# A graph layer with a mixture of experts on one core: statistics moved, matmuls of constants added, small tables relocated

## The reference

```python
xn  = layernorm(x)
h   = einsum('ni,roi->rno', xn, weight)            # 8 relations
x   = x + segment_sum(h[edge_type, src], dst) + bias
xn2 = layernorm(x)
p   = softmax(xn2 @ gate_w + gate_b)               # 16 experts
top 2 of p, normalised to sum 1                    # per node
x   = x + sum over the two: p_e * ((silu(xn2 @ w1[e]) * (xn2 @ w2[e])) @ w3[e])
```

## Time and profile before

| | us |
|---|---|
| three runs | 925.81, 927.80, 933.22 (median 927.8) |
| the profiled execution | 927.84 |
| its span | 926.1 |
| PE busy | 725.9 (78%) |
| POOL busy | 659.9 (71%) |
| DVE busy | 520.1 (56%) |
| ACT busy | 300.0 (32%) |

### The profile page before, as it was taken

How to read it: one execution, slowest core, us unless ns; L and a number is a source line. 1 busy time by engine, 2 the same in 40 slices (tenths; PEclk the granted TensorE clock), 3 DMA queues, 4 the chain that set the end, 5 groups by cost and what they waited for, 6 DMA issues and landing times.

```text
span 926.1 us, 17827 instructions
## 1 busy us (share of the span) xinstructions
PE 725.9 (78%) x4528; PEld 617.5 (67%) x4529; DVE 520.1 (56%) x1447; ACT 300.0 (32%) x466; POOL 659.9 (71%) x614
## 2 busy tenths in 40 slices
PE   0135778888887898877889887388999999999980
PEld 0123567666776677766777666267888888888870
DVE  6687746465454654546554577883444444344438
ACT  5423233252222433234332333222333333233323
POOL 7774777777777777777777760249788796987772
PEclk9997799899998999989999999589999999999995
DMA  9872444454444433343334334166756664763546
GB/s 207 245 224 63 146 145 145 144 178 145 144 144 137 133 104 103 106 130 107 102 106 131 106 95 147 34 203 236 222 186 227 205 197 167 229 210 95 158 135 188
DMA packets 91487, 141.91 MB, mean 153 GB/s; under 512 B 13197, under 2 KB 65889, under 8 KB 91456
## 3 DMA queue, kind: packets, MB, share of 16 engines
q0 software_dynamic: 25680, 70.16, 26.2%
q1 hardware_dynamic: 48854, 56.28, 18.9%
q10 hardware_dynamic: 16922, 15.15, 5.1%
HBM read 108.61 MB, written 32.93 MB: 153 GB/s over the span
## 4 chain that ended last, share of the span: by engine, by line
PE 39%; POOL 25%; issue 17%; DMA 11%; DVE 3%; ACT 2%; SPq 1%; DVEq 1%; POOLq 0%; ACTq 0%
POOL got L573 21%; PE ps L1677 15%; PE ps L1659 8%; PE ps L1525 8%; DMA got<-x_tab,gidx 5%; PE ps L1537 5%; DMA acc<-in_x 2%; PE ps L1685 2%; POOL x_sb L618 2%; DMA store<-in_L_gnn_weight 2%; PE ps L1643 1%; DVE ps L1450 1%; POOL part L607 1%; DMA y_tab<-ffn 1%; DMA x_tab<-x_sb 1%
## 5 line engine op out<-in xcount | busy, mean ns | idle before, releaser
L573 POOL DMA_INDIRECT got<-x_tab,gidx x388 | 370.9, 956 | 127.1 <-issue 113.1
L1525 PE MATMUL ps<-hot,got 125*128 125x256 f16 x1700 | 222.0, 292 | 88.3 <-DMA got<-x_tab,gidx 69.7
L1525 PEld LDWEIGHTS ps<-hot,got 125*128 125x128 f16 x1700 | 172.9, 104 | 133.2 <-issue 45.9
L1095 DVE TENSOR_TENSOR store<-store,ps 128x512 f32 x150 | 102.6, 684 | 187.8 <-PE ps L1525 153.2
L1677 PE MATMUL ps<-part,operands 128*128 x696 | 180.7, 409 | 5.3 <-POOL part L607 4.1
L1537 PE MATMUL ps<-part,store 128*128 128x256 f32 x800 | 183.7, 388 | 0.5 <-DVE acc L1106 0.5
L1537 PEld LDWEIGHTS ps<-part,store 128*128 128x128 f32 x800 | 154.0, 195 | 21.0 <-issue 0.5
L1677 PEld LDWEIGHTS ps<-part,operands 128*128 128x128 f32 x696 | 129.6, 193 | 33.4 <-issue 6.1
L1077 DVE TENSOR_SCALAR hot<-key_row,pass,drel 125x256 f16<-125x256 f16 x425 | 124.4, 358 | 11.2 <-issue 11.1
L1659 PE MATMUL ps<-part,operands 128*128 x696 | 97.8, 289 | 3.2 <-DVE operands L1389 3.2
L607 POOL TENSOR_TENSOR part<-store,part 128x2048 fp32r<-128x2048 f32 (+1 forms) x28 | 98.0, 3499 | 2.3
(11 more groups left out here) (250 smaller groups left out, 658.0 us busy)
## 6 DMA issues: line engine op xcount, KB each, us to landing
store<-in_L_ffn_w SPq DMA_DIRECT2D x48, 512.0 KB
y_tab<-ffn SPq DMA_DIRECT2D x9, 896.0 KB, 4.5
y_tab<-ffn ACTq DMA_DIRECT2D x58, 128.0 KB
xs_tab<-x_sb SPq DMA_DIRECT2D x14, 512.0 KB, 3.2
ffn<-xs_tab ACTq DMA_DIRECT2D x55, 128.0 KB
got<-x_tab,gidx POOLq DMA_INDIRECT x388, 2.7
acc<-in_x SPq DMA_DIRECT2D x5, 560.0 KB
x_tab<-got SPq DMA_DIRECT2D x5, 560.0 KB
```

The source lines that it names most:

```text
L573: nc.gpsimd.indirect_dma_start(got[:, c, :], None, x_tab, bass.IndirectOffsetOnAxis(ap=gidx[:, col:col + 1], axis=0)).then_inc(gathered[g] ...
L1095: v.tensor_tensor(window, window, ps[:, WIN_BANK[g], :].rearrange("p (q n) -> p q n", n=WIN), ALU.add).then_inc(win_added, 1)
L1525: last = mm(ps[:, WIN_BANK[g], k * KEYS:(k + 1) * KEYS], got[0:CE, c, a * DIM + k * P:a * DIM + (k + 1) * P], hot[0:CE, g % HOT, c - c0, : ...
```

## The change

1. The 37 early gathers raise three semaphores: `held_in[0]` for the first ten, `[1]` for the next fifteen, `[2]` for the twelve of the odd turns. DVE takes the statistics of the first ten (`held_moments(0)`) and then `edge_keys()` ahead of `statistics(3)`; the other two parts stay where all 37 stood.
2. ACT, not DVE, copies the two lines of ends and the keys out of PSUM (semaphore `lines_kept`), behind its rows of x. DVE waits for the lines before it works on them and for the keys before L1033.
3. ACT takes the two square roots of the held rows in the midst of its eight copies of turned weights, behind the fourth, and waits there for all 37 variances (`held_var`).
4. DVE reads its counts into registers behind the held variances, ahead of its wait for these square roots.
5. `held_low(v0)` of the first turn of a sweep stands behind the first three windows' adds.
6. PE multiplies constants (`ones_h` with `key_row`, 128x128 by 128x256 float16, into a PSUM bank that nothing reads) at four places of routing: 28, 28, 20 and 22 times (`keep_clock`).
7. `oct_tables` stands behind the first tile's product; the rows `upto`, `upto_i` and `need` (now `slots_needed`) stand together ahead of the second tile's product; the result's weights and `pos2` stand behind the second tile.

```diff
+SOON = 10
+HELD_PARTS = (0, SOON, TILES, EARLY)
...
-                    bass.IndirectOffsetOnAxis(ap=early_idx[:, t:t + 1], axis=0)).then_inc(held_in, 16)
+                    bass.IndirectOffsetOnAxis(ap=early_idx[:, t:t + 1], axis=0)).then_inc(held_in[(t >= SOON) + (t >= TILES)], 16)
...
+            turned = "p (j q) -> p j q"
+            act.wait_ge(edges_turned, 2)
+            for n, ends_line in enumerate((lo_line, hi_line)):
+                nc.scalar.copy(ends_line.rearrange("p (q j) -> p j q", j=EJ),
+                               ps[0:1, 2 + n, 0:CHUNKS].rearrange(turned, j=EJ)).then_inc(lines_kept, 1)
+            nc.scalar.copy(key_c[0:CE, :].rearrange("p (q j) -> p j q", j=EJ),
+                           ps[0:CE, 1, 0:CHUNKS].rearrange(turned, j=EJ)).then_inc(lines_kept, 1)
+
             for n in range(8):
                 k, rp = n // 4, n % 4
                 act.wait_ge(w_turned, n + 1)
                 nc.scalar.copy(wT[:, k, rp * QW:(rp + 1) * QW], ps[:, 5 + n % 3, :]).then_inc(wT_ready, 1)
+                if n == 3:
+                    act.wait_ge(held_var, EARLY)
+                    nc.scalar.activation(dev[0:CE, :], mv[0:CE, :, 1], ACT.Sqrt, bias=eps[0:CE, 1:2], scale=SCALE ** -2).then_inc(held_dev, 1)
+                    nc.scalar.activation(odd_dev[0:CE, :], odd_mv[0:CE, :, 1], ACT.Sqrt, bias=eps[0:CE, 1:2], scale=SCALE ** -2).then_inc(held_dev, 1)
...
+            def held_moments(part):
+
+                t0, t1 = HELD_PARTS[part:part + 2]
+                dve.wait_ge(held_in[part], (t1 - t0) * 16)
+                for t in range(t0, t1):
+                    n = t - TILES
+                    v.bn_stats((stat[0:CE, t, :] if n < 0 else odd_stat[0:CE, n, :]),
+                               (held[0:CE, t, :] if n < 0 else odd_held[0:CE, n, :])).then_inc(held_stats, 1)
+                for t in range(t0, t1):
+                    n = t - TILES
+                    dve.wait_ge(held_stats, t + 1)
+                    v.bn_aggr((mv[0:CE, t, :] if n < 0 else odd_mv[0:CE, n, :]),
+                              (stat[0:CE, t, :] if n < 0 else odd_stat[0:CE, n, :])).then_inc(held_var, 1)
+
...
             for n in range(1, X_LOADS):
+                if n == 3:
+                    held_moments(0)
+                    edge_keys()
                 statistics(n)
-                if n == 3:
-                    edge_keys()
...
-            step(v.tensor_copy(key_c[0:CE, :].rearrange("p (q j) -> p j q", j=EJ), ps[0:CE, 1, 0:CHUNKS].rearrange(turned, j=EJ)))
-            for n, ends_line in enumerate((lo_line, hi_line)):
-                step(v.tensor_copy(ends_line.rearrange("p (q j) -> p j q", j=EJ), ps[0:1, 2 + n, 0:CHUNKS].rearrange(turned, j=EJ)))
+            dve.wait_ge(lines_kept, 2)
...
+            held_moments(1)
+            held_moments(2)
+            dve.wait_ge(counts_ready, 5)
...
+            tiles_n = dve.value_load(n_tiles[0:1, 0:1], min_val=1, max_val=TILES)
...
             dve.wait_ge(held_dev, 2)
...
-                    held_low(v0)
                     for g in range(HALF):
                         one_hots((g + HOT_AHEAD) // NG, (g + HOT_AHEAD) % NG)
                         add_window(v0, 0, g, w, 0, offs)
+                    held_low(v0)
...
+            def keep_clock(n):
+
+                for _ in range(n):
+                    mm(ps[:, IDLE_BANK, 0:KEYS], ones_h[:, :], key_row[:, :], start=True, stop=True)
+
+            keep_clock(28)
             pe.wait_ge(hots_done, 1)
             ranks(FIRST_PART, TILES).then_inc(ranks_done, 1)
+            keep_clock(28)
             pe.wait_ge(own_summed, 1)
...
+            keep_clock(20)
             by_hots = ([(k, t) for k in range(2) for t in range(HOT_TILES)] + [(k, t) for k in range(2) for t in range(HOT_TILES, TILES)])
...
             last.then_inc(inv_summed, 1)
+            keep_clock(22)
             pe.wait_ge(upto_kept, 2)
```

The tables between the expert tiles on DVE; `slots_needed` and `result_weights` hold the instructions that stood at L1415 to L1419 with L1436 to L1440, and at L1422 to L1433 with L1441:

```diff
                 if not first:
                     low_hid(j - 1)
+                    if tables:
+                        tables()
...
                 v.tensor_tensor(hid, gate, ps[:, UP_BANK + 1, :], ALU.mult).then_inc(hid_ready, 1)
+                if first and tables:
+                    tables()
                 low_xs(j + 1)
...
             split_first(0, (DOWN_PART,))
-            oct_tables()
-            expert_tile(0, 0, first=True)
+            expert_tile(0, 0, first=True, tables=oct_tables)
             split_first(1, (UP_PARTS, DOWN_PART))
-            expert_tile(0, 1)
+            expert_tile(0, 1, tables=slots_needed)
+            result_weights()
             expert_tile(1, 0)
             expert_tile(1, 1)
```

More of the change, by code:

```diff
@@ L286, in build @@
         early_rows = sem("early_rows")
-        early_turned = sem("early_turned")
         early_ready = sem("early_ready")
-        held_in = sem("held_in")
+        held_in = [sem(f"held_in{n}") for n in range(3)]
+        lines_kept = sem("lines_kept")
         held_stats = sem("held_stats")
@@ L989, in _ @@
                 low_row(t)
-            dve.wait_ge(edges_turned, 1)
+            dve.wait_ge(edges_turned, 2)
             turned = "p (j q) -> p j q"
@@ L1043, in _ @@
             v.memset(limit[:, :], 0.0).then_inc(edges_done, 1)
-            dve.wait_ge(held_in, EARLY * 16)
-            for t in range(EARLY):
-                n = t - TILES
-                v.bn_stats((stat[0:CE, t, :] if n < 0 else odd_stat[0:CE, n, :]),
-                           (held[0:CE, t, :] if n < 0 else odd_held[0:CE, n, :])).then_inc(held_stats, 1)
-            for t in range(EARLY):
-                n = t - TILES
-                dve.wait_ge(held_stats, t + 1)
-                v.bn_aggr((mv[0:CE, t, :] if n < 0 else odd_mv[0:CE, n, :]),
-                          (stat[0:CE, t, :] if n < 0 else odd_stat[0:CE, n, :])).then_inc(held_var, 1)
+            held_moments(1)
+            held_moments(2)
+            dve.wait_ge(counts_ready, 5)
+            dve.wait_ge(edges_done, 1)
+            dve.wait_ge(acc_init, 1)
+            dve.wait_ge(bias_kept, 1)
+            tiles_n = dve.value_load(n_tiles[0:1, 0:1], min_val=1, max_val=TILES)
+            wins_n = dve.value_load(n_wins[0:1, 0:1], min_val=1, max_val=GEN_W)
+            single = dve.value_load(single_i[0:1, 0:1], min_val=0, max_val=1)
+            visits = dve.value_load(n_visits[0:1, 0:1], min_val=TILES, max_val=TILES * TILES * GEN_W)
             dve.wait_ge(held_dev, 2)
@@ L1390, in low_hid, with expert_tile @@
                                 hidT[:, 0, :, :].bitcast(F32), ALU.subtract).then_inc(hidT_ready, 1)
-            def expert_tile(i, u, first=False):
+            def expert_tile(i, u, first=False, tables=None):
                 j = i * 2 + u
@@ L1409, in _ @@
             split_first(0, (DOWN_PART,))
-            oct_tables()
-            expert_tile(0, 0, first=True)
-            split_first(1, (UP_PARTS, DOWN_PART))
-            expert_tile(0, 1)
-            dve.wait_ge(upto_kept, 2)
-            TILE_ROW = [1, TILES, EXPERTS]
-            for k in range(2):
-                step(v.tensor_tensor(mine, upto_tile, bc(same[:, EXPERTS - 2 + k, :], TILE_ROW, 1), ALU.mult))
-                step(v.tensor_reduce(upto[:, k, :], mine, AX.X, ALU.add))
-            expert_tile(1, 0)
@@ L1429, in _ @@
-            step(v.tensor_tensor(wts[:, 1, :], wts[:, 1, :], wts[:, 0, :], ALU.mult))
-            for k in range(2):
-                v.tensor_tensor(wts2[:, k, :], wts[:, 0, :], is_low[:, k, :], ALU.mult)
-                step(v.tensor_tensor(mtx[:, :], wts[:, 1, :], is_low[:, 1 - k, :], ALU.mult))
-                step(v.tensor_tensor(wts2[:, k, :], wts2[:, k, :], mtx[:, :], ALU.add))
-            expert_tile(1, 1)
-            step(v.tensor_scalar(upto_i[:, :, :], upto[:, :, :], float(P - 1), None, ALU.add))
```

55 lines of the change are left out of this document (29 added, 26 removed).

## The result

The changed kernel took 919.12 us (median of 4 runs), the kernel before 927.45 beside it: a ratio of 0.9886, 95% interval 0.9859 to 0.9913. Predicted were 917.9 with a range of 915.0 to 922.0. One of the four runs took 937.93 at a lower granted clock (0.835, where the others had 0.93); the ratio leaves it out, and the other three have a median of 918.04. The profiled execution took 918.04, its span is 916.3; before they were 927.84 and 926.1.

What follows compares the result with a forecast made beforehand. POOL's stream of gathers was taken to bound the graph stage, with one hole of 9.17 us to close. 927.84 - 9.2 (hole) - 0.4 (constants) - 0.3 (tables) = 917.9 us, range 915.0 to 922.0.

Steps and rivals of the forecast that it cites:

- Ten statistics, "free": DVE's preparation: ten early held statistics, 4.1 us, fit its wait for batch 3; edge keys bring later rows 1.0 forward.
- Copies on ACT: Preparation: three copies, 2.75 us, leave DVE, which waits 0 for ACT and is 3.7 early with the edge keys' 1.0.
- Held rows at 65.2: DVE's preparation: the other 27 held rows take 6.1 and 4.9 us, ending at 65.2 and not 73.6.
- Square roots and DVE's loads: Preparation: DVE's 2.9 us of register loads run beside ACT's roots; ACT waits up to 1.0; clear ends at 73.4.
- Start of PE, 70.2: PE's first window starts at 70.2 through DVE's chain, against 71.1 needed; the hole closes, gain 9.17 us.
- Matmuls of constants, +0.4: Routing: constants raise PE's clock, 0.4 us won at the inverse table; ends 1.5 lost and 0.5 won.
- Rival C: Routing's first 28 constants at half clock: hole closed, DVE waits 1.5 for ranks, 920.1 us; chance 0.15 with E.
- Tables, +0.3: Expert stage: moved tables spare PE's idle before the seventh tile; 1.3 could be won, 1 lost; 0.3 us taken.
- A: Preparation: hole closes only in part, PE starts at 72 to 74, gain 6 to 8, 921 us; chance 0.20.
- B: Routing and experts: hole closes, clock stays full through the seventh tile's product, table early, 916.8 us; chance 0.12.
- D: Preparation: slower, DVE waits for ten gathers; decides if the tenth lands from 34.4, 935.4 us at 42; chance 0.03.
- E: Routing: clock stays at half despite the constants, only 0.4 and 0.3 go, 918.6 us; chance 0.15 with Rival C.

Runs made afterwards that it cites:

- ten_late_again: Changed kernel with the first ten held statistics back among the others, edge keys still ahead of batch 3, measured a second time: 920.77 us, ratio 0.9912.
- no_constants: Changed kernel without its 98 matmuls of constants: 918.30 us, ratio 0.9893 to the kernel before.
- reads_early: Changed kernel with PE's two register loads moved ahead of its turning of the weights: 918.74 us, ratio 0.9897 to the kernel before.
- old_tables: Changed kernel with the small tables at their places of before: 918.15 us, ratio 0.9897 to the kernel before.
- routing_only: Kernel before with only the matmuls of constants and the relocated tables: 929.58 us, ratio 1.0002 to the kernel before.

## Why the prediction was right

The forecast was 917.9 and the time 919.1 (918.0 without the long run). The main term, the hole in POOL's stream, is most of what was won: 7.5 of the 9.8 us of the span. That the sum came out within 0.1 in the span (916.2 and 916.3) is in part luck: the hole closed by 7.5 and not by 9.2, the constants and tables brought 0.1 and not 0.7 that can be traced to them, and what fills the gap are the 0.64 by which POOL's own first turn ended early and the 1.2 behind the first routed gather, neither of which the sum had. Point by point:

*The bound.* Right. POOL's stream of gathers sets the graph stage and the hole was the one thing in it to win. Where it closed fully (three kernels) the time is no better than where 1.35 were left: such a difference is less than the spread between runs of one kernel. From POOL's second turn to the choice pass 493.8 to 496.6 us in the eight traces, whatever the edits.

*Ten statistics, "free".* Partly wrong. The tenth gather landed at 25.4, not at 23.6, so that ten statistics and edge keys (7.0) ran to 32.4, past batch 3 at 29.75. "I take 1.0" for the rows behind it was 0.4 by the copy of the index (45.15 to 44.77). The upper bound, 2.0, is about what `ten_late_again` got by leaving the ten out (42.74, 2.4 early). The net worth of the ten is 1.8 at DVE, not 4.1, and they cost the issue of the weights' load 2.0.

*Copies on ACT.* Right: DVE waited 0.23 for them, and was 3.1 early at L1027 (49.01 to 45.90, with the 0.4), against 3.7 predicted.

*Held rows at 65.2.* 65.3 in the trace. DVE began them at 54.6 and not 54.2, and the 27 took 10.7 instead of 11.0.

*Square roots and DVE's loads.* Predicted was a wait of up to 1.0 on ACT for the variances. There was none, because the weights landed at 62.5. In `no_constants`, with a landing at 61.45, the fourth copy ends within 0.2 of the last variance (65.75 and 65.58). DVE's four loads took 2.18, not 2.9, and its one-hots began at 68.26, with no 0.3 for the head of the loop: by DVE alone PE could have started at 69.4. The clear ended at 75.09, not at 73.4, and "no one-hot does" need it is wrong: in DVE's queue the wait for it (L1262) stands ahead of the one-hots of the fourth group. In `reads_early` DVE idled 3.34 there and PE 1.65 in its first turn; POOL's gathers show no gap from it.

*Start of PE, 70.2.* It was 71.84, 70.43, 70.44 in the three executions with that preparation. The chain I named, through DVE, is not the one that decides; the other does: "PE's own two register loads stand behind the last copy ... 67.8 + 1.5 = 69.3, earlier". From the last copy to PE pass 2.33, not 1.5, and the last copy ended at 69.5, not at 67.8. `reads_early` shows the first: with only these loads moved, PE starts 1.1 nearer to the last copy (1.24 instead of 2.33) and waits for DVE. The second is the landing, 2.7 later than the 59.8 that the sum implies: issued 0.4 and not 1.0 early, and 16.7 underway where I had kept the 14.7 of before. In the eight traces this load took 13.8 to 16.7; with 14.7, by my estimate, PE would have started at 69.8 (45.75 + 14.7 + 9.3), or at 70.2 if ACT then waits for the variances, and the hole would have closed. So this part of the miss is chance. The hole's limit moved too: POOL's first turn ended 0.64 early, so that PE had to start by 70.5 and not by 71.1. 70.43 and 70.44 closed the hole, in `old_tables` with 0.1 to spare, and 71.84 left 1.35. The hole's term was 7.5 in the profiled execution (9.17 to 1.65), inside the ends 7.2 and 9.17 but 1.7 short of what I took.

*Matmuls of constants, +0.4.* The saving of 0.34 at the table is there in four executions of six, but the first 28 found the clock at half in every execution (4.88 to 6.01 us) and delayed the ranks by 0 to 0.85. Together, from the choice to `first_idx`, that is up to 0.3 won in five executions and 0.8 lost in one, so the term is near nil. Rival C's mechanism, half clock at the first 28, is what happens, at up to 0.85 instead of 1.5, and belonged in the forecast.

*Tables, +0.3.* The full clock at the seventh tile came, and is worth 1.3 in that product (4.34 to 3.04), but `old_tables` and `no_constants` have it as well. The 1.2 won behind the first routed gather are in all variants (0.8 to 1.8), in `routing_only` too, which is no faster than before; I can't tie them to an edit, and with one trace of the kernel before they may be its own spread.

*The rivals.* A (hole closed in part) is close to what the profiled execution did: PE at 71.84 and 7.5 won, where A has 72 to 74 and 6 to 8, and 1.35 left where its sign was 2. The cause was none of the waits that A names but the weights' load and PE's loads. B brought less than it promised, D needed the tenth gather at 34.4 and it came at 25.4, and E did not happen: the clock stood at 1.00 from 576 to 586.

*Which parts close the hole.* That the preparation as a whole does is shown by times and traces. Of its parts, none is told by its time alone. By the traces: the place of the square roots (an edit by itself, PE 6.7 nearer to the landing of the weights), and PE's register loads, which the change leaves in place and `reads_early` moves by themselves (1.1). Read from the trace without an edit of their own: DVE's register loads (2.9). The ten early statistics: a wait of 3.11 on ACT appears without them, but they are worth 1.8 on DVE at most, and nothing that the time shows. Argued only: the copies on ACT.

## What to carry to other kernels

When an engine that sets a stage shows one hole, price every edit elsewhere against that hole alone, and count each chain that ends at it, the sequencer's register loads too: here the second chain, on paper 0.9 ahead of the first, was the one that decided. Keep the time that a large load is underway as a range: here 13.8 to 16.7 us, a spread of 2.9 against the 0.9 of room that the sum had. Work moved into an idle stretch is free only if what stands next to it in that stretch still fits; here 7.0 us were put into 4.3, and the rows behind came 0.4 early instead of 2.4. A releaser that a trace names can be the wrong one: a gap of the same size in traces where the named engine was done long before is the engine's own. Matmuls that were to raise the clock ran at half clock themselves until it rose (the first 28 here, 4.9 to 6.0 us for 3.2), and the real ones queued behind them paid for that.

## What the runs showed that I had not expected

Twenty-eight matmuls of 256 columns at the same place took 4.88, 5.17, 5.34, 5.35, 5.41 and 6.01 us in six executions, one each of six kernels that hold them, where 28 at full clock take 3.22, and the last fourteen of the inverse table 0.58 in four executions and 0.93 in two (`reads_early` and `routing_only`), though the same 76 constants ran ahead of them. The clock also fell to half right behind the table in the changed kernel, between 586 and 587, after ten microseconds at full clock in which PE was busy for about 5.5 (3.23 in 578 to 584, 1.44 and 0.86 in the two windows beside), while 22 constants ran behind one another: they took 4.23, and 2.35 is what 20 took at full clock. The Trainium skill ("TensorE: Matmul & The Clock Gate", Part 1, the HAM clock gate) says that the gate's beat is free-running, so that the same kernel counts different numbers of slow matmuls from run to run. These traces agree as far as they go (4.88 to 6.01), but no kernel was traced twice in the same condition.

The relation weights landed at 59.74 to 62.98 in eight executions. A part of that is their issue, at 43.7 to 47.2, which the edits move; but from issue to landing they took 13.8 to 16.7 us, a spread as large as DVE's register loads were worth. And in two groups of runs waits ended 0.5 to 2.5 us late, and the kernel before took 1186 to 1188 us in place of 930: only kernels measured side by side can be set against each other.
